# A four-slot transformer kernel: the late stages of each slot run among the attention units, on four engines

## Time and profile before

| | |
|---|---|
| time, median of 3 runs | 1054.31 us (1053.47 to 1058.15) |
| time of the profiled execution | 1054.93 us |
| its span, first to last instruction | 1053.1 us |
| busy: PE, DVE, ACT, POOL | 880.1, 594.5, 352.0, 177.2 us |
| mean granted TensorE clock | 0.896 of full |
| first attention unit on DVE begins | 657.12 us |
| last attention unit on DVE ends | 894.17 us |

### The profile page before, as it was taken

One profiled execution on the slowest core, in us unless ns is written; L12 is line 12 of the kernel. 1 busy time (PEld: TensorE's weight loads), 2 busy tenths in 40 slices (PEclk: granted clock), 3 DMA queues, 4 the chain that ended last, 5 costly groups with the idle time before them and its releaser, 6 DMA issues.

```text
span 1053.1 us, 13422 instructions
## 1 busy us (share of the span) xinstructions
PE 880.1 (84%) x4751; PEld 647.6 (61%) x4751; DVE 594.5 (56%) x2021; ACT 352.0 (33%) x675; POOL 177.2 (17%) x220
## 2 busy tenths in 40 slices
PE   7999999999999999968649996587776766546997
PEld 5886777777777999854328874354544444433444
DVE  8983321211213452577661025999999999785431
ACT  1005443334334222210001211575556676211210
POOL 4101000000101000020110011455444454110000
PEclk9999999999999999958779987887869998757997
DMA  9500000000000256500001300000000000000000
GB/s 367 221 1 1 2 1 1 1 1 1 1 1 1 103 199 250 210 1 0 0 1 70 141 1 0 1 1 1 1 1 1 1 1 1 0 1 0 1 11 30
DMA packets 5042, 42.79 MB, mean 41 GB/s; under 512 B 496, under 2 KB 1520, under 8 KB 2288
## 3 DMA queue, kind: packets, MB, share of 16 engines
q1 hardware_dynamic: 4976, 41.94, 10.5%
HBM read 40.89 MB, written 1.05 MB: 40 GB/s over the span
## 4 chain that ended last, share of the span: by engine, by line
PE 63%; DVE 22%; issue 7%; POOL 5%; ACT 2%; DMA 0%; DVEq 0%; POOLq 0%; ACTq 0%
PE PB L648 11%; PE PB L637 10%; PE PB L764 5%; PE PB L950 4%; POOL arena L535 3%; DVE X L1773 3%; PE PB L602 3%; PE PB L592 2%; DVE arena L1946 2%; PE PB L1165 2%; PE PB L1154 2%; PE PB L1047 2%; DVE top L1951 2%; DVE arena L1954 2%; PE PB L551 2%
## 5 line engine op out<-in xcount | busy, mean ns | idle before, releaser
L1644 DVE SCALAR_TENSOR_TENSOR X<-PB,comb,X 128x128 f32<-128x128 f32 x128 | 36.0, 345 | 167.1 <-PE PB L648 167.1
L1266 ACT ACTIVATE arena<-PB,arena 128x512 f32<-128x512 f32 x128 | 87.4, 687 | 120.2 <-PE PB L637 120.1
L648 PEld LDWEIGHTS PB<-arena 128*128 128x128 f32 x1024 | 118.5, 192 | 11.0 <-issue 10.4
L648 PE MATMUL PB<-arena 128*128 128x128 f32 x1024 | 119.9, 276 | 0.0
L637 PE MATMUL PB<-XN,arena 128*128 128x512 f32 x256 | 115.6, 594 | 2.2 <-ACT arena L1266 2.2
L437 POOL TENSOR_TENSOR lnrs<-lnve,mhalf 128x4 f32<-128x4 f32 x32 | 32.6, 1020 | 479.9 <-DVE lnve L1525 479.2
L535 POOL TENSOR_TENSOR arena<-arena 128x512 f32<-128x512 f32 x64 | 81.5, 1273 | 119.2 <-ACT arena L1431 119.2
L1029 PE MATMUL PB<-ring 128*128 128x256 f32 x256 | 78.0, 434 | 22.2 <-ACT arena L1426 21.9
L1097 PE MATMUL PB<-w_first,arena 128*128 128x128 f32 x256 | 47.2, 314 | 45.6 <-POOL arena L535 45.5
L1216 ACT ACTIVATE XN<-PB 128x512 f32<-128x512 f32 x28 | 16.6, 594 | 184.2 <-PE PB L551 184.2
L637 PEld LDWEIGHTS PB<-XN,arena 128*128 128x128 f32 x256 | 46.1, 190 | 49.3 <-issue 44.6
(11 more groups left out here) (241 smaller groups left out, 1516.9 us busy)
## 6 DMA issues: line engine op xcount, KB each, us to landing
ring<-in_taps_dram SPq DMA_DIRECT2D x12, 1536.0 KB, 7.0
ring<-in_taps_dram SPq DMA_DIRECT2D x7, 1792.0 KB, 7.2
arena<-in_stage_dram SPq DMA_DIRECT2D x1, 4176.0 KB, 22.9
w_later<-in_later_dram SPq DMA_DIRECT2D x1, 2951.5 KB, 13.5
XN<-in_x_dram SPq DMA_DIRECT2D x4, 256.0 KB, 5.6
out_dram<-XN SPq DMA_DIRECT2D x4, 256.0 KB, 2.1
arena<-in_mods_dram SPq DMA_DIRECT2D x1, 534.0 KB, 23.8
w_first<-in_first_dram SPq DMA_DIRECT2D x1, 271.0 KB, 2.7
```

Of the source, the lines that this page charges most:

```text
L648: last = mm(PB[3 + d % 2][:, t * P:t * P + P], H[d % 2][hc][:, t * P:t * P + P], W["W2"][:, d % E, hc, :], start=hc == 0, stop=hc == 3)
L1266: A(H[d % 2][c % 4], PB[c % 3][:], ACT.Gelu, bias=W["b1"][:, c % 32:c % 32 + 1])\
```

## The change

The last three parts are rearranged so that each slot's work follows its own last unit at fixed distances, on every engine. With `d = c - 16*(s+1)` the step counted from the end of slot s's units, `follow(s, d)` names what slot s does at step d; later slots come first within a step, and `follow` stands ahead of the unit on DVE and POOL, behind it on PE and ACT. The loop runs over 64 + 36 steps; those after 63 have no unit.

- The rounding of slots 0, 1 and 2, the routers and experts of slots 0 and 1 now stand within the 64 steps. The rounding stays on DVE as a whole, shorter by one instruction. For slots 0 and 1 an expert product takes two steps, for slots 2 and 3 one. Each slot has its own router.
- `ln_apply` for the last three norms moves from DVE to POOL.
- The positions become three accumulated products on PE with diagonal matrices (`posd`, made by POOL), and ACT adds the bias. The copy of v moves to ACT; its bias, through `Wo`, goes into `bo` once. The next slot's projections stand in steps 1 to 6 of every eight (slots 1, 2, 3 begin at steps 0, 8, 16).
- `Silu` on ACT and one product on DVE become `Tanh(x/2)` on ACT and two `scalar_tensor_tensor` on DVE.
- The router finds the two best by `MAX8` and `MATCH_REPLACE8` per tile in place of twelve whole-width instructions; this holds for all three routers of the kernel.
- `pv` uses one bank for both halves of a slot, the other banks are given out anew.

```diff
+TAIL = 36
...
+        posd = ringf[:, 5 * NTOK + 512:5 * NTOK + 512 + 3 * P].rearrange("p (i c) -> p i c", i=3)
...
+            def ln_apply(n, s):
+                ln_pow(n, s)
+                pool.wait_ge(*at(ln_rstd[n], s + 1))
+                for t in range(TILES * s, TILES * s + TILES):
+                    last = g.tensor_scalar(XT[:, t, :], X[:, t, :], lnmv[:, t, 0:1], lnrs[:, t:t + 1],
+                                           ALU.subtract, ALU.mult)
+                last.then_inc(xt_ready[n][0], 1)
...
-            ln_pow(5, 0)
+            for i in range(3):
+                last = g.tensor_scalar(posd[:, i, :], ident, W["posw"][:, i:i + 1], None, ALU.mult)
...
+            ln_apply(5, 0)
+            pool.wait_ge(setup_dve, 4)
...
+            def follow(s, d):
+                if d == 7:
+                    ln_apply(6, s)
+                elif d == 12:
+                    std(s)
+                elif d == 17:
+                    ln_apply(7, s)
...
+            for c in range(UNITS + TAIL):
+                for s in range(1, SLOTS):
+                    if c == 8 * (s - 1):
+                        ln_apply(5, s)
+                    if c == 8 * (s - 1) + 2:
+                        shift(2, 5, s, W["bo"])
+                for s in reversed(range(SLOTS)):
+                    follow(s, c - 16 * (s + 1))
+                if c >= UNITS:
+                    continue
...
+                if s == 0:
+                    mm(PB[3][:, 0:C], W["bvT"], W["Wo"], start=True, stop=True).then_inc(setup_pe, 1)
...
+            def positions(s, bank):
+                pe.wait_ge(*at(xn_ready[5], s + 1))
+                pe.wait_ge(fills, 7)
...
+                mm(bank[:], posd[:, 1, :], xn(s), start=True, stop=False)
+                mm(dst[:, :, 1:HW], posd[:, 0, :], src[:, :, 0:HW - 1], start=False, stop=False)
+                mm(dst[:, :, 0:HW - 1], posd[:, 2, :], src[:, :, 1:HW], start=False, stop=True).then_inc(pos_done, 1)
...
+            def next_slot(s, i):
...
+                    ln_turn(5, s, PB[7])
...
+                    positions(s, PB[7])
+                elif i == 3:
+                    pe.wait_ge(xp_ready, s + 1)
+                    project(s, 0, PB[7])
+                elif i in (4, 5):
+                    pe.wait_ge(qk_ready, 2 * s + i - 3)
+                    project(s, i - 3, PB[7])
...
+                mm(gate[:], W["Wgate"][:, i, :], xn(s), start=True, stop=True).then_inc(gate_done, 1)
+                mm(up[:], W["Wup"][:, i, :], xn(s), start=True, stop=True).then_inc(upp_done, 1)
...
+            def follow(s, d):
+                if d == -4:
+                    pe.wait_ge(po_ready, 2 * s + 1)
...
+                    turn(PB[2], lambda t: PO[2 * (s % 2)][:, t * P:t * P + P], po_turned)
+                elif d == 2:
+                    pe.wait_ge(po_ready, 2 * s + 2)
...
+                    turn(PB[2], lambda t: PO[2 * (s % 2) + 1][:, t * P:t * P + P], po_turned)
+                elif d == 4:
+                    pe.wait_ge(ot_ready, 2 * s + 2)
+                    turn(PB[2], lambda t: XT[:, TILES * s + t, :], ot_turned)
+                elif d == 5:
+                    pe.wait_ge(oc_ready, s + 1)
...
+                elif d == 8:
...
+                    ln_turn(6, s, PB[4])
+                elif d == 9:
+                    rotate(s, PB[4])
+                elif d == 10:
+                    square_sums(s, PB[4])
+                elif d == 18:
+                    pe.wait_ge(ms_ready, s + 1)
+                    ln_turn(7, s, PB[4])
+                elif d == 19:
+                    logits(2, 7, s, W["Wg3"], PB[4])
+                elif d == 22:
+                    pe.wait_ge(router_shifted, GROUPS_BEFORE[2] + s + 1)
+                    comb_turn(2, s, s, PB[4])
+                if s < 2:
+                    if d in (19, 21, 23, 25, 27):
+                        gate_up(s, (d - 19) // 2)
+                    if d in (24, 26):
+                        comb_pairs(s, (d - 24) // 2)
+                    if d == 29:
+                        comb_pairs(s, 2)
+                        comb_pairs(s, 3)
+                    if d == 31:
+                        moe_down(s)
+                    if d == 33:
+                        turn_final(s)
+                else:
+                    if 19 <= d <= 23:
+                        gate_up(s, d - 19)
+                    if 23 <= d <= 26:
+                        comb_pairs(s, d - 23)
+                    if d == 27:
+                        moe_down(s)
+                    if d == 28:
+                        turn_final(s)
+
+            ln_turn(5, 0, PB[3])
+            positions(0, PB[2])
+            pe.wait_ge(xp_ready, 1)
+            project(0, 0, PB[0])
+            project(0, 1, PB[1])
+            project(0, 2, PB[2])
...
+            for c in range(UNITS + TAIL):
+                if c + 2 < UNITS:
+                    lg(c + 2)
+                if c < UNITS:
+                    pe.wait_ge(sub_ready, c + 1)
+                    if c >= 1:
+                        pe.wait_ge(pt_ready, c)
...
+                if c % 4 == 0 and 0 < c <= UNITS:
+                    pv(c // 4 - 1)
+                for s in range(1, SLOTS):
+                    next_slot(s, c - 8 * (s - 1))
+                for s in reversed(range(SLOTS)):
+                    follow(s, c - 16 * (s + 1))
...
+            def position_copy(s, bank):
+                act.wait_ge(pos_done, s + 1)
+                A(XP, bank[:], ACT.Identity, bias=W["posw"][:, 3:4]).then_inc(xp_ready, 1)
...
+            def gate_tanh(s, i):
...
+                A(SG[c % 2], PB[6 if s < 2 else [6, 0][i % 2]][:], ACT.Tanh, scale=0.5).then_inc(tanh_done, 1)
...
+            def follow(s, d):
+                if d == -6:
+                    po_copy(s, 0)
+                elif d == 2:
+                    po_copy(s, 1)
+                elif d == 5:
+                    oc_copy(s)
+                elif d == 9:
+                    ln_copy(6, s, PB[4])
+                elif d == 10:
+                    had_copy(s, PB[4])
+                elif d == 19:
+                    ln_copy(7, s, PB[4])
+                elif d == 21:
+                    router_act(2, s, (s,))
+                elif d == 23:
+                    comb_copy(2, s, PB[4])
+                if s < 2:
+                    if d in (20, 22, 24, 26, 28):
+                        gate_tanh(s, (d - 20) // 2)
+                    if d == 34:
+                        final_copy(s)
...
...
+                if 1 <= c <= UNITS:
+                    pt_copy(c - 1)
...
+            def router_start(r, group, slots, bank, gamma=None):
...
+                dve.wait_ge(logits_done, SLOTS * r + slots[-1] + 1)
...
+                link(v.tensor_reduce(q(0), lg, AX.X, ALU.max))
+                v.tensor_tensor(R(0), lg, q(0).unsqueeze(2).to_broadcast([P, n, E]), ALU.subtract)\
+                 .then_inc(router_shifted, 1)
+
+            def router_finish(r, group, slots, renorm=False):
...
+                for t in range(n):
+                    k = mark(v.max(R(4)[:, t, :], R(3)[:, t, :]))
+                after(k)
+                link(v.memset(R(4)[:, :, 2:E], -1.0))
+                for t in range(n):
+                    k2 = mark(v.match_replace(R(5)[:, t, :], R(4)[:, t, :], R(3)[:, t, :], 0.0))
...
+                    v.tensor_tensor(comb[:, tiles, :], R(3), R(5), ALU.subtract).then_inc(comb_ready, 1)
...
+            def round4(s):
...
+                dve.wait_ge(std_ready, s + 1)
+                link(v.tensor_scalar(q(3), q(2), 2.513930578568423, 1e-8, ALU.mult, ALU.add))
+                v.tensor_scalar(q(7), q(3), -1.0, None, ALU.mult)
+                v.tensor_scalar(q(8), q(2), TRUST, None, ALU.mult)
+                link(v.tensor_scalar(q(4), q(3), 2.0 / 15.0, None, ALU.mult))
+                v.tensor_scalar(q(6), q(4), 0.5, None, ALU.mult)
+                link(v.reciprocal(q(5), q(4)))
+                dve.wait_ge(had_sq, s + 1)
+                after(by_image(s, h1, HS[s], 3, 7, ALU.min, ALU.max))
+                after(by_image(s, h1, h1, 5, 0.5, ALU.mult, ALU.add))
+                link(v.tensor_scalar(h1, h1, MAGIC, -MAGIC, ALU.add, ALU.add))
+                after(by_image(s, h1, h1, 4, 6, ALU.mult, ALU.subtract))
+                link(v.tensor_tensor(h2, h1, HS[s], ALU.subtract))
+                v.scalar_tensor_tensor(h2, h2, -1.0, h2, ALU.mult, ALU.max).then_inc(error_ready, 1)
+
+            def add_rounded(s):
...
+                after(by_image(s, h2, h2, 8, None, ALU.is_le))
+                link(v.tensor_tensor(h2, HS[s], h2, ALU.mult))
+                link(v.tensor_tensor(h3, h1, h2, ALU.subtract))
+                link(v.tensor_tensor(h3, h2, h3, ALU.add))
+                v.tensor_tensor(xf(s), xf(s), h3, ALU.add).then_inc(x_rounded, 1)
+
+            def gated(s, i):
...
+                dve.wait_ge(tanh_done, c + 1)
```

(113 more changed lines are left out.)

539 lines of the change are left out of this document (184 added, 355 removed).

## The result

The changed kernel takes 1063.11 us (median of 8 runs, 1060.16 to 1064.54) against 1054.11 (8 runs, 1052.68 to 1058.15): ratio 1.0081, interval 1.0067 to 1.0095. It is slower by 0.8%; the forecast was 1048, 0.6% faster. The profiled execution took 1063.33, its span is 1061.5. Ratios here are of fast runs alone, so one execution of e9b that took 2261.54 us stands in none.

A forecast was written before the change was run, and what follows sets the result against it. DVE was taken to bound the loop, a chain from engine to engine the end. Start 657.5, loop 304.7 and end 84.0 gave a span of 1046.2 us, written as a time of 1048; range 1024 to 1070 (8 in 10).

The forecast's parts named there:

- Parts 1 and 2: DVE's work in the loop: 206.2 us remain after what leaves, and 62.6 us enter.
- Part 3: New DVE waits in the loop, for ACT, logits and PE's products: 35.9 us (bounds 14 and 60).
- Other `pv` steps 1.: In the loop, waits at the remaining steps with a value product: 1 us in all.
- Part 4: The start, ahead of the first unit: net +0.4 us (bounds -2 and +3), first unit at 657.5.
- Part 5: The end, behind the last unit: 84.0 us (bounds 74 and 98) in place of 158.9.
- (a): In the end, from the last unit through `moe_down(1)`, `pv`, turns and copies to the logits: about +15 us.
- (b): In the end, slot 2's experts mixed with slot 3's output product, norm and Hadamard product: 40.5 us taken, `round4(3)` behind `add_moe(2)`.
- (c): In the end, slot 3 alone, from its rounding to the output: 43.5 us.
- A: Rival: the loop's new waits fall together, 18 us in place of 36, end 82, time 1028; chance 0.26.
- B: Rival: PE at the lower clock bounds early steps and end; waits 27 for 12, end 92, time 1071; chance 0.22.
- C: Rival: `Tanh` shares no table with `Exp`, loads in the loop cost up to 25.6 us, time 1074; chance 0.05.

The follow-up runs named there:

- e9b: Changed kernel with division, `add_attention`, combines and `add_moe` of slots 0 and 1 behind the unit on DVE, gates and router still ahead: 1053.55 us, ratio 0.9978.
- e6: Changed kernel with DVE's late stages behind the unit, the end's three norm applications on DVE, and `add_moe(2)` behind `round4(3)`: 1018.75 us, ratio 0.9665.
- e7: Changed kernel with POOL's norm application in three forms (two pointer scalars, one pointer and a constant, one operation alone), values differ: 1061.13 us, one execution.
- e3: Changed kernel with the three norm applications behind the last unit made by DVE in place of POOL: 1060.45 us, ratio 1.0068.
- e8: Changed kernel with DVE's late stages behind the unit and every application of norms 5 (slots 1 to 3), 6 and 7 on DVE: 1031.8 us, ratio 0.9805.

## Why the prediction was wrong

**Parts 1 and 2, right.** DVE's time without waits came out at 268.7 against 268.8. The rounding of slot 0, in the loop, took 768.10 to 774.14 and 777.74 to 782.50, 10.8 us (10.75 forecast); slot 3's, alone, 1013.66 to 1022.13 = 8.47 (8.55). The contention is there: L1988, with two tiles in SBUF, takes 1.65 us in the loop and 0.69 in the end. But it is wider than the earlier trace rows show, for instructions that read one tile are hit as well. The four clips of slot 0's rounding beside POOL's subtraction, and those of slot 3 alone:
```profile
769.31 2.23 DVE L1962 TENSOR_SCALAR arena<-arena,hst 128x256 f32<-128x256 f32 x4
```
```profile
1014.47 1.39 DVE L1962 TENSOR_SCALAR arena<-arena,hst 128x256 f32<-128x256 f32 x4
```
So 0.84 of the slot's 2.3 us is here and 0.40 at L1971 (0.57 for 0.17). The rule of the Trainium skill (SBUF — State Buffer, Who interferes with whom) names both kinds, two SBUF inputs and the 2-port modes that a `tensor_scalar` can enter, and agrees in kind; the gate products and combines, with one input in PSUM, stayed at 0.69 or less even where POOL worked beside the whole of one. The size was the trace's 2.3 a slot, not the 3.2 that I worked out from the rule.

**Part 3, the counted waits, right.** Timeline of the kernel after at c = 37, answering: ACT's second exponential of the unit just ended, the copy, the tanh behind them, and on DVE the gate product that waits for it.
```profile
806.98 0.91 ACT L1544 ACTIVATE arena<-arena,nmx 128x256 f32<-128x256 f32 x2 [0.60 <-DVE arena L2079]
...
807.79 0.57 ACT L1458 ACTIVATE arena<-PB 128x512 f32<-128x512 f32 x1
...
808.27 0.58 ACT L1485 ACTIVATE arena<-PB 128x512 f32<-128x512 f32 x1
808.89 0.69 DVE L1997 SCALAR_TENSOR_TENSOR arena<-arena,PB 128x512 f32<-128x512 f32 x1 [1.62 <-ACT arena L1485]
```
Six gates wait 1.62, 2.85, 3.65 and again 1.62, 2.87, 3.65, with 0.8 more on the second product: 17.1 against 15.2 forecast. The router's 4.1 (4.7), `add_moe(0)` 3.8 (3), and the logits with the early steps 9.2 (12) came near their prices.

**Part 3, the step that failed: "Other `pv` steps 1."** I named the waits of four kinds of instruction and took all others as covered, at 1 us in all. They cost 13.8: the divisions 6.5, `add_attention` 3.5, the combines 2.9, the mean square 0.9. The longest, at c = 14, timeline of PE and DVE:
```profile
702.86 0.66 PE L1254 MATMUL PB<-w_first,arena 128*128 128x128 f32 x4 [0.60 <-POOL arena L562]
...
703.45 1.92 PE L1073 MATMUL PB<-arena,ring 128*32 128x256 f32 x16
...
705.30 1.12 PE L1040 MATMUL PB<-ring,w_later 128*128 128x512 f32 x2
...
706.26 0.60 PE L570 MATMUL PB<-w_first,arena 128*128 128x128 f32 x4
...
706.90 0.26 DVE L1938 RECIPROCAL rdn<-PB 128x16 f32<-128x16 f32 x1 [3.41 <-PE PB L570]
707.19 0.42 DVE L1939 TENSOR_TENSOR XT<-PB,rdn 128x256 f32<-128x256 f32 x1
707.53 0.75 DVE L2065 MAX8 top<-PB 128x8 f32<-128x256 f32 x2
```
PE turns the values at step 12 and DVE divides them at step 14. Two steps sound like 6 us of room, but PE gets to step 12 only when POOL has subtracted for the unit just ended, at +2.4, and before the turn that the division needs stand, in order, a turn, the `pv` of 1.92 and the next slot's projection; DVE is through with unit 13, and at the division, at +3.0. The granted clock from 698 to 708 us is 1.00, so this wait is not the clock's. The same arithmetic that I made for the tanh (release by the unit just ended, plus what stands ahead in the queue) gives this wait; I made it for ACT and not for PE. In e9b these calls but the mean square, with `add_moe`, stand behind the unit, and the loop is 13.0 us shorter; the whole miss in the loop is 12.1.

**Part 4, mis-sized, in our favour by 3.6.** Starts of the profiled executions scatter by 5 us, so this term says little.

**Part 5, (a) and (b), mostly right.** `round4(3)` stood behind `add_moe(2)` as forecast, at +43.0 (40.5). The end of the kernel after, PE, DVE and POOL:
```profile
1006.73 6.29 PE L1163 MATMUL PB<-w_later,arena 128*128 128x128 f32 x40 [0.78 <-DVE arena L2007]
...
1013.06 0.69 DVE L2011 TENSOR_TENSOR X<-X,PB 128x512 f32<-128x512 f32 x1 [6.31 <-PE PB L1163]
1013.66 0.16 DVE L1970 TENSOR_SCALAR hst<-hst 128x2 f32<-128x2 f32 x1
...
1022.13 0.87 DVE L1576 BATCH_NORM_STATS2 lnst<-X 128x6 f32<-128x128 f32 x4
...
1023.57 1.01 POOL L441 TENSOR_TENSOR lnrs<-lnve,mhalf 128x4 f32<-128x4 f32 x1 [16.02 <-DVE lnve L1582]
1024.68 3.12 POOL L447 TENSOR_SCALAR XT<-X,lnmv,lnrs 128x128 f32<-128x128 f32 x4
1027.94 1.09 PE L570 MATMUL PB<-w_first,XT 128*128 128x128 f32 x4 [13.48 <-POOL XT L447]
```
The 6.29 of PE is `moe_down(2)`, between the 4.73 and 7.22 of the earlier trace rows. e6 shows that the order, not PE, made slot 3 wait for it: I forecast the wait and left it as given, though DVE had ready work behind.

**Part 5, (c), the second mis-sized term.** 47.8 in place of 43.5. POOL's four applications took 3.12, not 1.2, and above the upper bound as well: I had taken 0.71 each from the earlier trace rows, an instruction four times as wide but with one pointer scalar, and thought width to be the price. It is the kind of operand (e7). The sum was also written down wrong: the terms of (c) add to 43.1, so 4.7 are to be explained. The time up to the applied norm took 14.1 for 12.3, from there to the first gate product 6.4 for 5.2, gates, router and combines 16.0 for 13.8, `moe_down(3)` 6.7 for 7.2. From the rounding to the first gate product the granted clock was 0.58: PE is busy 6.2 of these 20.5 us, and its turn takes 1.09 there and 0.66 in the earlier trace rows.

**The rivals.** A fell: the waits added up. C fell: no table is loaded in the loop, as the page of the Trainium skill had it (ScalarE: Activation LUTs, Table sets: the hidden batching unit). B was right in sign and wrong in cause for the loop, 15 of its 23 us: it decides from a clock under 0.75 in the first third of the loop, and that window of the kernel after shows 0.85:
```profile
653.90:759.50 105.60, 79.42 (x386) 51.41 (x384) 87.81 (x379) 66.27 (x147) 62.85 (x71) 0.85 0.00 1
```
In e9b, besides, 13 us of the loop went at an unchanged clock. B's other half, an end of 92, came near (90.8), and in the last stretch a lower clock is indeed worth some 2 us (e3, e7); but POOL's applications are 1.9 of that end, too. The slower case that came true, DVE idle behind its own queue head in more places than I had counted, was none of the rivals; its waits, 48.1, lay within my bounds of 14 and 60, and its time within the range.

## What to carry to other kernels

On an in-order engine that bounds a loop, put a consumer behind the loop's own unit, not ahead of it, when its producer on another engine is released by the unit just ended: here this turned a loss of 0.8% into a gain of 2%, with no work removed. When distances between stages are cut, work out for every consumer when its producer comes out of its own queue, not only for those with a new producer. Ahead of waits, extra work on the bound engine is partly free, behind them it costs in full, so remove the waits before judging any other edit.

## What the runs showed of the hardware

- POOL, 128x128 in float32: two pointer scalars 0.79 us, one pointer and a constant 0.37, one pointer with a single operation 0.605. At 512 columns the form with a pointer and a constant takes 0.71. Four of the two-pointer form in a row take 3.12 on POOL and 1.12 on DVE.
- DVE in the loop of e8, beside POOL's subtractions: the same application takes 0.37 in the mean, 1.34 at most, and in the end 0.34.
- In the kernel after, a DVE `TENSOR_SCALAR` within SBUF that begins while POOL's 1.27 us subtraction runs ends only behind it, small ones too: the one of 128x4 in the statistics (L1582) takes 0.87 in the mean and up to 1.22 in the loop, alone 0.17. The seven of them in the loop lose 4.9 us, more than the clips of three slots; much of it is no new cost, for the kernel before has six in its loop (L1525, 4.1 us).
- `MAX8` on 8 elements takes 0.156 us and `MATCH_REPLACE8` 0.152; the finish of a router of four tiles took 2.5 us in the loop and 2.1 in the end, where 2.4 was taken.
